# Cross-attention kernel: the low part of the context columns made by a negating copy on ScalarE and an accumulating DMA, in place of three VectorE subtractions

## Chip, cores and metric

One core of a Trainium2 chip runs the program. The metric is the device time of one execution in microseconds (us). The kernel before took 1278.85 us (median of three runs, 1278.84 to 1280.06).

## What is computed

The reference is one cross-attention layer over 64 batch elements, each with 256 text rows x (512 wide) and 256 context rows (384 wide):

```
text_p  = H_l @ W_text  + b_text          # [256, 512]
audio_p = H_a @ W_audio + b_audio         # [256, 512]
Q = layer_norm(text_p,  g1, beta1);  K = layer_norm(audio_p, g2, beta2);  V = audio_p
alpha   = softmax(Q @ K^T / sqrt(512))
H_hyper = (alpha @ V) @ W_out + b_out
return layer_norm(H_hyper + H_l, g_out, beta_out)
```

Inputs and output are float32.

## The kernel before

The 64 batch elements are taken in pairs: 32 steps, and in each step all matrix work is done on 512 tokens. Steps 0, 1, 30 and 31 are written out; steps 2 to 29 are a loop whose body holds two steps (`run_steps`). Every engine has its own program, and all order between engines is by semaphores written out by hand; there is no planner. The order of the calls inside each engine's `step` is the order of its queue.

TensorE multiplies in a rounded 32-bit format. To keep the precision of float32, each operand is split in a high part (a rounded copy) and a low part (the value less its high part), and each product is three matmuls: high by high, high by low, low by high. The context columns `cT_in` (128 partitions, 3 chunks of 512 tokens, 768 KB) are such an operand: `cT_hi` and `cT_lo` feed the K projection, `project_k`, with which each step of TensorE begins.

Step i on TensorE: `project_k` (4 banks), `project_q` (4 banks) with `mean_squares` of K in the middle of bank 1, `probs_context` of step i-1, `output_part` of step i-1 with `mean_squares` of Q in between, and `scores`. So at the end of a step TensorE goes straight from the scores of step i to `project_k` of step i+1, which needs `cT_hi` and `cT_lo` of step i+1. In the kernel before `product` waits for them chunk by chunk, on `cT_split` (one count for each VectorE subtraction).

How the parts of the context columns come about in step i, for step i+1:

- ScalarE makes `cT_hi` chunks 0 and 1 (`cT_high`) behind `move_half` of K, in front of `y_norm(i-2, odd, 0)` and of `rstd_of` for K; chunk 2 late in the step, behind `xT_minus`.
- VectorE makes `cT_lo` (`cT_low`): chunk 0 in front of the four `k_norm`, chunk 1 behind the last `q_low`, chunk 2 in front of `maxima(i, 0)`.
- SyncE then loads `cT_in` for step i+2 (`load_cT`), behind a wait on `cT_split`; `store_p`, `load_p` and the other transfers of the step are queued behind that wait.

For x the kernel already does otherwise: ScalarE makes all of `xT_hi` and then `xT_lo = -xT_hi` (`xT_minus`), and a GpSimd DMA adds `xT_in` to it (`add_xT`, accumulating, 1024 KB), after which `xT_split` counts 16. Only in step 0 does VectorE subtract (`x0_low`). GpSimd's queue in a step: `scales` and `finish_y(.., 0)` of step i-2, `pair_squares`, `bias_x` (an accumulating DMA of 1024 KB that adds the output bias to y rows), `finish_y(.., 1)`, `add_xT`, four `split_c`, `finish_y(.., 2)` and `(.., 3)`.

The stretch of ScalarE's step that the prediction follows is: `move_half` of Q, `k_high(i, 3)`, `pc_high(j, 1)`, `pc_high(j, 2)`, `rstd_of` for Q. `pc_high` rounds two of three banks of the probabilities-by-context product; VectorE's `pc_low(j, 1)`, `pc_low(j, 2)`, `k_low(i, 3)`, then `q_norm` and `q_low` follow it, and `scores` waits for the four `q_low`.

Of the kernel before, what the change touches and what calls it, by code (L numbers as in the profile page):

```python
# [18 lines left out]
def cross_attention_kernel(nc, x_rows, xT, c_rows, cT, w_text, b_text, w_audio, b_audio, w_out, b_out,  # L19
# [13 lines left out]
    with ExitStack() as stack:  # L33
# [92 lines left out]
        k_moved, q_moved = sem("k_moved"), sem("q_moved")  # L126
        k_log, q_log, k_rstd, q_rstd = sem("k_log"), sem("q_log"), sem("k_rstd"), sem("q_rstd")
        xT_negated, x0_split = sem("xT_negated"), sem("x0_split")
        k_centred, k_squared = sem("k_centred"), sem("k_squared")
        q_centred, q_squared, y_normed = sem("q_centred"), sem("q_squared"), sem("y_normed")  # L130
        kT_hi_made, qT_hi_made = sem("kT_hi_made"), sem("qT_hi_made")
# [53 lines left out]
        def _(sp):  # L185
# [46 lines left out]

            def step(i, odd, first=False, last=False):
                if first:
                    wait_apart(sp, cT_split, CT)
                    load_cT(1)
                    sp.wait_ge(x0_split, DT)
                elif not last:
                    wait_apart(sp, xT_split, 16 * i)
                if last:  # L240
                    sp.wait_ge(xT_split, 16 * (N - 1))
                    sp.dma_start(last_rows[:], x_rows[N - 1]).then_inc(x_last, 16)
                else:
                    load_xT(i + 1)
                if first:
                    sp.wait_ge(wao_done, CT)
                elif isinstance(i, int) and i == 1:
                    sp.wait_ge(bao_done, 1)
                if not isinstance(i, int) or i >= 2:
                    for t in (0, 1):  # L250
                        store_y(i - 2, odd, t)
                if not isinstance(i, int) or i < N - 2:
                    wait_apart(sp, cT_split, CT * (i + 2))
                    load_cT(i + 2)
                if not last:
                    store_p(i)
                if not isinstance(i, int) or i >= 2:
                    for t in (2, 3):
                        store_y(i - 2, odd, t)
                if not last:  # L260
                    load_p(i)
                for t in range(0 if last else T):
                    if not isinstance(i, int) or i >= 2:
                        wait_apart(sp, stored[t], 16 * (i - 1))
                    load_x(i, odd, t)
# [16 lines left out]
        def _(pe):  # L282
# [19 lines left out]
            def project_k(i, h):  # L302

                if isinstance(i, int) and i == 0:
                    pe.wait_ge(waT_copied, h + 1)
                wait(pe, y_summed, T * (i - 2) + h + 1)
                cols = slice(h * P, (h + 1) * P)
                terms = [(wa_hi[:, d, cols], wa_lo[:, d, cols], cT_hi[:, d, :], cT_lo[:, d, :]) for d in range(CT)]
                at_begin = isinstance(i, int) and i == 0 and h == 0
                product(wide[h][:], terms, cT_split if h == 0 else None, CT * i,  # L310
                        wa_split if at_begin else None).then_inc(k_done, 1)

            def project_q(i, h, part=None):
# [189 lines left out]
        def _(act):  # L503
# [6 lines left out]
            def xT_minus(i):  # L510

                act.wait_ge(xT_hi_made, DT * (i + 1))
                nc.scalar.mul(xT_lo[:], xT_hi[:].bitcast(F32), -1.0).then_inc(xT_negated, 1)  # L513

            def c_high(i):
                act.wait_ge(c_loaded, 16 * (i + 1))
                wait(act, pc_done, CT * i)
                nc.scalar.copy(c_hi[:], c_kept[:]).then_inc(c_hi_made, 1)  # L518
# [118 lines left out]
            def step(i, odd, first=False, last=False):  # L637
# [14 lines left out]
                if not last:  # L652
                    cT_high(i + 1, 0)
                    cT_high(i + 1, 1)
                if late:
                    y_norm(i - 2, odd, 0)
                rstd_of(i, turn[0], k_var, k_log, k_rstd)
# [10 lines left out]
                    pc_high(j, 0)  # L668
                move_half(i, turn[1], q_summed, q_moved)
                k_high(i, 3)  # L670
                if first:
                    wao_high(0)
                    wao_high(1)
# [18 lines left out]
                    wao_high(2)  # L692
                if not last:
                    xT_minus(i + 1)
                    cT_high(i + 1, 2)
                c_high(i)
                if late:
                    y_norm(i - 2, odd, 2)
# [48 lines left out]
        def _(dve):  # L747
# [6 lines left out]

            def cT_low(i, d):
                dve.wait_ge(cT_hi_made, CT * i + d + 1)
                low(cT_lo[:, d, :], cT_in[:, d, :], cT_hi[:, d, :]).then_inc(cT_split, 1)

            def turn_p(j):

# [194 lines left out]
            def step(i, odd, first=False, last=False):  # L955
# [13 lines left out]
                if late:  # L969
                    y_gain(i - 2, odd, 1)  # L970
                    y_gain(i - 2, odd, 2)
                if not last:
                    cT_low(i + 1, 0)
                k_norm(i, 0)
                k_norm(i, 1)
                k_norm(i, 2)
# [27 lines left out]
                if first:  # L1004
                    wao_low(2)
                    make_bao()
                if not last:
                    cT_low(i + 1, 1)
# [3 lines left out]
                if not last:  # L1012
                    cT_low(i + 1, 2)
                maxima(i, 0)
                if last:
                    wide_sum(y_rows[1 - odd], j, 2)
# [58 lines left out]
        def _(pool):  # L1075
# [21 lines left out]
            def add_xT(i):  # L1097

                wait_apart(pool, xT_negated, i)
                nc.gpsimd.dma_start(xT_lo[:], xT_in[:], accum_op=ALU.add).then_inc(xT_split, 16)  # L1100

            def split_c(i, t):

                if t == 0:
# [47 lines left out]
            def step(i, odd, first=False, last=False):  # L1152
# [12 lines left out]
                    bias_x(j, 1 - odd)  # L1165
                if last:
                    bias_last()
                if late:
                    finish_y(i - 2, odd, 1)
                if not last:  # L1170
# [60 lines left out]
```

## Time and profile before

| | |
|---|---|
| median of three runs | 1278.85 us |
| profiled execution, its own time | 1279.1 us |
| its span, first to last instruction | 1277.3 us |
| mean granted TensorE clock | 0.997 |
| TensorE matmul busy | 1257.2 us, 98% |
| VectorE busy | 1078.8 us, 84% |
| ScalarE busy | 1054.7 us, 83% |
| GpSimd busy | 547.5 us, 43% |
| DMA moved | 253.53 MB, mean 198 GB/s |

In the rows PE is TensorE's matmul, PEld its weight load (which runs beside the matmul before it), DVE VectorE, ACT ScalarE, POOL GpSimd, SPq the queue of SyncE, and L523 line 523 of the kernel. Helpers that write one kind of instruction for many tiles have one line (L749 is every subtraction), so go by the names of the tiles. Names in the trace are merged for likewise named tiles: "score<-kT_hi,qT_hi" is the matmul of `scores`. A matmul's end is modelled, so the starts of matmuls and weight loads are what tells TensorE's pace.

### The profile page before, as it was taken

To read this page: it belongs to the slowest core of one execution; us is meant where nothing else is said; L and a number is where in the kernel's file an instruction comes from. 1 tells how busy PE (TensorE), PEld (TensorE's weight loads), DVE (VectorE), ACT (ScalarE), POOL (GpSimd) and SP (SyncE) were. 2 spreads that over 40 slices of the span, in tenths; PEclk is the share of its full clock that TensorE was granted. 3 is DMA by queue.
4 is the path that set the end of the run, shared out by engine and by line. 5 is a ranking of instruction groups with operands and counts; after the bars stand their busy time and mean duration, and the time that the engine had idled before them with its cause. 6 is when DMAs were issued, how large, how long until landed. Compare 5 with 4: busy or idle time off the path is not lost.

```text
span 1277.3 us, 22559 instructions
## 1 busy us (share of the span) xinstructions
PE 1257.2 (98%) x6648; PEld 1066.4 (83%) x6648; DVE 1078.8 (84%) x1726; ACT 1054.7 (83%) x1789; POOL 547.5 (43%) x545
## 2 busy tenths in 40 slices
PE   6999999999999999999999999999999999999997
PEld 5688888888888888888888888888888888888886
DVE  6678888988888988888888888888889888889888
ACT  6777888888888888888888888888888888888874
POOL 0113554335544335544345544345544355543356
PEclk9999999999999999999999999999999999999999
DMA  7257766768766678766678667688666687667693
GB/s 255 60 162 224 225 191 182 186 202 238 227 169 198 184 216 238 212 178 194 182 227 238 204 170 194 192 234 231 185 187 184 202 243 222 179 189 188 209 233 105
DMA packets 99013, 253.53 MB, mean 198 GB/s; under 512 B 12336, under 2 KB 28208, under 8 KB 90800
## 3 DMA queue, kind: packets, MB, share of 16 engines
q1 hardware_dynamic: 77632, 187.22, 41.8%
q0 software_dynamic: 21360, 66.06, 28.7%
q8 instruction: 10, 0.16, 0.1%
q14 instruction: 11, 0.09, 0.0%
HBM read 137.38 MB, written 49.81 MB: 147 GB/s over the span
## 4 chain that ended last, share of the span: by engine, by line
PE 96%; DVE 2%; ACT 1%; DMA 1%; SPq 1%; issue 0%; ACTq 0%; DVEq 0%
PE wide L326 9%; PE wide L327 9%; PE wide L325 9%; PE score L293 7%; PE score L292 7%; PE score L294 7%; PE wide L294 7%; PE wide L292 7%; PE wide L293 7%; PE wide L382 7%; PE wide L381 7%; PE wide L380 7%; PE turn L334 2%; PE turn L293 1%; PE turn L294 1%; PE turn L292 1%
## 5 line engine op out<-in xcount | busy, mean ns | idle before, releaser
L1123 POOL TENSOR_TENSOR y_rows<-y_rows,betao_row 128x512 f32<-128x512 f32 x120 | 167.0, 1391 | 337.9 <-ACT y_rows L585 226.3
L325 PE MATMUL wide<-xT_hi,wt_hi 128*128 128x512 f32 x512 | 202.5, 395 | 3.4 <-ACT k_cols L545 3.4
L326 PE MATMUL wide<-xT_lo,wt_hi 128*128 128x512 f32 x512 | 202.5, 396 | 0.0
L327 PE MATMUL wide<-xT_hi,wt_lo 128*128 128x512 f32 x512 | 202.5, 396 | 0.0
L292 PE MATMUL wide<-cT_hi,wa_hi 128*128 128x512 f32 x384 | 151.7, 395 | 0.7 <-DVE wa_lo L924 0.7
L544 ACT ACTIVATE squares<-wide,bac_col 128x512 f32<-128x512 f32 x128 | 88.3, 690 | 77.2 <-PE wide L294 77.0
L294 PE MATMUL wide<-cT_hi,wa_lo 128*128 128x512 f32 x384 | 151.6, 395 | 0.0
L293 PE MATMUL wide<-cT_lo,wa_hi 128*128 128x512 f32 x384 | 151.3, 394 | 0.0
L382 PE MATMUL wide<-wao_hi,pcT_lo 128*128 128x512 f32 x372 | 146.7, 394 | 0.0
L380 PE MATMUL wide<-wao_hi,pcT_hi 128*128 128x512 f32 x372 | 146.6, 394 | 0.0
L381 PE MATMUL wide<-wao_lo,pcT_hi 128*128 128x512 f32 x372 | 146.5, 394 | 0.0
L292 PE MATMUL score<-kT_hi,qT_hi 128*128 128x256 f32 x512 | 145.3, 284 | 1.0 <-DVE qT_lo L825 1.0
L294 PE MATMUL score<-kT_hi,qT_lo 128*128 128x256 f32 x512 | 144.7, 283 | 0.0
L293 PE MATMUL score<-kT_lo,qT_hi 128*128 128x256 f32 x512 | 144.7, 283 | 0.0
L1106 POOL TENSOR_TENSOR c_lo<-c_kept,c_hi 128x384 fp32r<-128x384 f32 x128 | 126.1, 1011 | 19.5 <-ACT c_hi L518 19.5
L1100 POOL DMA_DIRECT2D xT_lo<-xT_in x31 | 27.8, 897 | 233.7 <-ACT xT_lo L513 233.7
L325 PEld LDWEIGHTS wide<-xT_hi,wt_hi 128*128 128x128 f32 x512 | 96.9, 189 | 25.6 <-ACT k_cols L545 4.3
L326 PEld LDWEIGHTS wide<-xT_lo,wt_hi 128*128 128x128 f32 x512 | 96.7, 189 | 22.8
L327 PEld LDWEIGHTS wide<-xT_hi,wt_lo 128*128 128x128 f32 x512 | 96.8, 189 | 22.4
L576 ACT ACTIVATE qT_hi<-q_cols,beta_col 128x512 fp32r<-128x512 f32 x128 | 90.7, 725 | 28.1 <-DVE q_cols L819 25.4
L825 DVE SCALAR_TENSOR_TENSOR qT_lo<-q_cols,beta_col,qT_hi 128x512 fp32r<-128x512 f32 x128 | 102.6, 801 | 8.5
L819 DVE SCALAR_TENSOR_TENSOR q_cols<-q_cols,g_col,turn 128x512 f32<-128x512 f32 x128 | 92.0, 740 | 12.4 <-ACT turn L567 12.4
(145 smaller groups left out, 3515.6 us busy)
## 6 DMA issues: line engine op xcount, KB each, us to landing
xT_in<-in_xT SPq DMA_DIRECT2D x32, 1024.0 KB, 9.0
xT_lo<-xT_in POOLq DMA_DIRECT2D x31, 1024.0 KB, 8.9
y_rows<-in_x_rows SPq DMA_DIRECT2D x124, 256.0 KB, 4.0
y_rows<-bao_row POOLq DMA_DIRECT2D x31, 1024.0 KB, 9.4
out<-y_rows SPq DMA_DIRECT2D x124, 256.0 KB, 3.3
cT_in<-in_cT SPq DMA_DIRECT2D x32, 768.0 KB, 8.7
c_kept<-in_c_rows SPq DMA_DIRECT2D x32, 768.0 KB, 7.5
p_out<-probs SPq DMA_DIRECT2D x31, 512.0 KB, 4.6
```

Of the source, the lines that this page charges most:

```text
L292: nc.tensor.matmul(to, a_hi, b_hi, start=(m == 0), stop=False)
L293: nc.tensor.matmul(to, a_hi, b_lo, start=False, stop=False)
L294: done = nc.tensor.matmul(to, a_lo, b_hi, start=False, stop=(m == n - 1))
L325: nc.tensor.matmul(wide[h][:], wt_hi[:, d, cols], xT_hi[:, d, :], start=(d == 0), stop=False)
L326: nc.tensor.matmul(wide[h][:], wt_hi[:, d, cols], xT_lo[:, d, :], start=False, stop=False)
L327: done = nc.tensor.matmul(wide[h][:], wt_lo[:, d, cols], xT_hi[:, d, :], start=False, stop=(d == DT - 1))
L380: nc.tensor.matmul(wide[t][:], hi, wao_hi[:, d, :], start=(d == 0), stop=False)
L381: nc.tensor.matmul(wide[t][:], hi, wao_lo[:, d, :], start=False, stop=False)
L382: done = nc.tensor.matmul(wide[t][:], lo, wao_hi[:, d, :], start=False, stop=(d == CT - 1))
L825: nc.vector.scalar_tensor_tensor(out=lo[:, h, :], in0=cols[:, h, :], scalar=shift[:, h:h + 1], in1=hi[:, h, :].bitcast(F32), op0=ALU.add, ...
L1106: nc.gpsimd.tensor_tensor(c_lo[:, t, :], c_kept[:, t, :], c_hi[:, t, :].bitcast(F32), ALU.subtract).then_inc(c_split, 1)
L1123: nc.gpsimd.tensor_tensor(rows, rows, betao_row[:], ALU.add).then_inc(y_ready, 1)
```

## The change

ScalarE makes the third chunk of `cT_hi` together with the other two, early in the step; `cT_minus`, one instruction over all three chunks (1536 elements in each partition), writes `-cT_hi` to `cT_lo` behind `k_high(i, 3)` and in front of `pc_high(j, 1)`; and a GpSimd DMA, `add_cT`, adds `cT_in` (768 KB) to it, queued between `bias_x` and `finish_y(i-2, odd, 1)`. The three VectorE subtractions of each step but the last are gone. Columns of step 0 are still split by VectorE, under a semaphore of their own, `c0_split`. `cT_split` now counts 16 for each DMA; TensorE waits for it once, ahead of `project_k(i, 0)`, and SyncE waits for it ahead of `load_cT`.

```
--- before.py
+++ after.py
@@ -126,6 +126,7 @@
         k_moved, q_moved = sem("k_moved"), sem("q_moved")
         k_log, q_log, k_rstd, q_rstd = sem("k_log"), sem("q_log"), sem("k_rstd"), sem("q_rstd")
         xT_negated, x0_split = sem("xT_negated"), sem("x0_split")
+        cT_negated, c0_split = sem("cT_negated"), sem("c0_split")
         k_centred, k_squared = sem("k_centred"), sem("k_squared")
         q_centred, q_squared, y_normed = sem("q_centred"), sem("q_squared"), sem("y_normed")
         kT_hi_made, qT_hi_made = sem("kT_hi_made"), sem("qT_hi_made")
@@ -232,7 +233,7 @@
 
             def step(i, odd, first=False, last=False):
                 if first:
-                    wait_apart(sp, cT_split, CT)
+                    sp.wait_ge(c0_split, CT)
                     load_cT(1)
                     sp.wait_ge(x0_split, DT)
                 elif not last:
@@ -250,7 +251,7 @@
                     for t in (0, 1):
                         store_y(i - 2, odd, t)
                 if not isinstance(i, int) or i < N - 2:
-                    wait_apart(sp, cT_split, CT * (i + 2))
+                    wait_apart(sp, cT_split, 16 * (i + 1))
                     load_cT(i + 2)
                 if not last:
                     store_p(i)
@@ -307,7 +308,9 @@
                 cols = slice(h * P, (h + 1) * P)
                 terms = [(wa_hi[:, d, cols], wa_lo[:, d, cols], cT_hi[:, d, :], cT_lo[:, d, :]) for d in range(CT)]
                 at_begin = isinstance(i, int) and i == 0 and h == 0
-                product(wide[h][:], terms, cT_split if h == 0 else None, CT * i,
+                if h == 0 and not at_begin:
+                    pe.wait_ge(cT_split, 16 * i)
+                product(wide[h][:], terms, c0_split if at_begin else None, 0,
                         wa_split if at_begin else None).then_inc(k_done, 1)
 
             def project_q(i, h, part=None):
@@ -512,6 +515,11 @@
                 act.wait_ge(xT_hi_made, DT * (i + 1))
                 nc.scalar.mul(xT_lo[:], xT_hi[:].bitcast(F32), -1.0).then_inc(xT_negated, 1)
 
+            def cT_minus(i):
+
+                act.wait_ge(cT_hi_made, CT * (i + 1))
+                nc.scalar.mul(cT_lo[:], cT_hi[:].bitcast(F32), -1.0).then_inc(cT_negated, 1)
+
             def c_high(i):
                 act.wait_ge(c_loaded, 16 * (i + 1))
                 wait(act, pc_done, CT * i)
@@ -652,6 +660,7 @@
                 if not last:
                     cT_high(i + 1, 0)
                     cT_high(i + 1, 1)
+                    cT_high(i + 1, 2)
                 if late:
                     y_norm(i - 2, odd, 0)
                 rstd_of(i, turn[0], k_var, k_log, k_rstd)
@@ -668,6 +677,8 @@
                     pc_high(j, 0)
                 move_half(i, turn[1], q_summed, q_moved)
                 k_high(i, 3)
+                if not last:
+                    cT_minus(i + 1)
                 if first:
                     wao_high(0)
                     wao_high(1)
@@ -692,7 +703,6 @@
                     wao_high(2)
                 if not last:
                     xT_minus(i + 1)
-                    cT_high(i + 1, 2)
                 c_high(i)
                 if late:
                     y_norm(i - 2, odd, 2)
@@ -754,7 +764,7 @@
 
             def cT_low(i, d):
                 dve.wait_ge(cT_hi_made, CT * i + d + 1)
-                low(cT_lo[:, d, :], cT_in[:, d, :], cT_hi[:, d, :]).then_inc(cT_split, 1)
+                low(cT_lo[:, d, :], cT_in[:, d, :], cT_hi[:, d, :]).then_inc(c0_split, 1)
 
             def turn_p(j):
 
@@ -969,8 +979,6 @@
                 if late:
                     y_gain(i - 2, odd, 1)
                     y_gain(i - 2, odd, 2)
-                if not last:
-                    cT_low(i + 1, 0)
                 k_norm(i, 0)
                 k_norm(i, 1)
                 k_norm(i, 2)
@@ -1004,13 +1012,9 @@
                 if first:
                     wao_low(2)
                     make_bao()
-                if not last:
-                    cT_low(i + 1, 1)
                 if not first:
                     y_sum(j, 1 - odd, 0)
                     y_sum(j, 1 - odd, 1)
-                if not last:
-                    cT_low(i + 1, 2)
                 maxima(i, 0)
                 if last:
                     wide_sum(y_rows[1 - odd], j, 2)
@@ -1099,6 +1103,11 @@
                 wait_apart(pool, xT_negated, i)
                 nc.gpsimd.dma_start(xT_lo[:], xT_in[:], accum_op=ALU.add).then_inc(xT_split, 16)
 
+            def add_cT(i):
+
+                wait_apart(pool, cT_negated, i)
+                nc.gpsimd.dma_start(cT_lo[:], cT_in[:], accum_op=ALU.add).then_inc(cT_split, 16)
+
             def split_c(i, t):
 
                 if t == 0:
@@ -1165,6 +1174,8 @@
                     bias_x(j, 1 - odd)
                 if last:
                     bias_last()
+                if not last:
+                    add_cT(i + 1)
                 if late:
                     finish_y(i - 2, odd, 1)
                 if not last:
```

## Rows read from the trace of the kernel before

**Rows 1.** The page: engines (busy us, share, instructions); chain that ended last.

```profile
PE 1257.2 (98%) x6648; PEld 1066.4 (83%) x6648; DVE 1078.8 (84%) x1726; ACT 1054.7 (83%) x1789; POOL 547.5 (43%) x545
PE 96%; DVE 2%; ACT 1%; DMA 1%; SPq 1%; issue 0%; ACTq 0%; DVEq 0%
```

**Rows 2.** Waits of TensorE: us in total, times, longest us.

```profile
PE wide L325 <- ACT k_cols L545: 3.4, 2, 2.0
...
PE score L292 <- DVE qT_lo L825: 1.0, 2, 0.7
```

**Rows 3.** Groups by line, whole trace: busy us, mean ns, idle before.

```profile
L749 DVE TENSOR_TENSOR cT_lo<-cT_in,cT_hi 128x512 fp32r<-128x512 f32 x96 | 66.0, 687 | 25.6 <-ACT cT_hi L523 25.6
...
L513 ACT ACTIVATE xT_lo<-xT_hi 128x2048 fp32r<-128x2048 f32 x31 | 59.4, 1916 | 1.0
...
L518 ACT CAST c_hi<-c_kept 128x1536 fp32r<-128x1536 f32 x32 | 47.2, 1475 | 0.0
```

**Rows 4.** Timeline of ScalarE in a loop step: start us, duration us, [idle before].

```profile
608.46 1.14 ACT L523 CAST cT_hi<-cT_in 128x512 fp32r<-128x512 f32 x2
...
611.00 0.66 ACT L565 ACTIVATE turn<-turn,eps 128x512 f32<-128x512 f32 x1 [0.77 <-PE turn L334]
...
621.44 0.57 ACT L539 CAST pcT_hi<-score 128x512 fp32r<-128x512 f32 x1
622.32 0.59 ACT L539 CAST pcT_hi<-turn 128x512 fp32r<-128x512 f32 x1 [0.32 <-PE turn L294]
623.94 0.66 ACT L565 ACTIVATE turn<-turn,eps 128x512 f32<-128x512 f32 x1 [1.03 <-PE turn L334]
```

**Rows 5.** Timeline of VectorE in the same step.

```profile
622.89 0.69 DVE L749 TENSOR_TENSOR pcT_lo<-score,pcT_hi 128x512 fp32r<-128x512 f32 x1
...
624.10 0.74 DVE L825 SCALAR_TENSOR_TENSOR kT_lo<-k_cols,beta_col,kT_hi 128x512 fp32r<-128x512 f32 x1
625.25 1.41 DVE L819 SCALAR_TENSOR_TENSOR q_cols<-q_cols,g_col,turn 128x512 f32<-128x512 f32 x2 [0.40 <-ACT turn L567]
...
630.55 0.75 DVE L825 SCALAR_TENSOR_TENSOR qT_lo<-q_cols,beta_col,qT_hi 128x512 fp32r<-128x512 f32 x1
```

**Rows 6.** Timeline of TensorE's weight loads in the same step.

```profile
610.46 0.19 PEld L334 LDWEIGHTS turn<-sq_parts,mean_of 128*128 128x128 f32 x1 [0.36 <-DVE sq_parts L749]
...
624.89 0.19 PEld L380 LDWEIGHTS wide<-wao_hi,pcT_hi 128*128 128x128 f32 x1
...
631.65 0.19 PEld L292 LDWEIGHTS score<-kT_hi,qT_hi 128*128 128x128 f32 x1
...
636.33 0.19 PEld L292 LDWEIGHTS wide<-cT_hi,wa_hi 128*128 128x128 f32 x1
```

**Rows 7.** Timeline of GpSimd in the same step.

```profile
616.53 1.35 POOL L1113 DMA_DIRECT2D y_rows<-bao_row  x1 [1.13 <-DMA y_rows<-in_x_rows]
625.93 1.30 POOL L1123 TENSOR_TENSOR y_rows<-y_rows,betao_row 128x512 f32<-128x512 f32 x1 [8.04 <-ACT y_rows L585]
```

**Rows 8.** DMA: landing of all 31 of line L1100 (xT_lo); the page's line of y_rows (KB each, us).

```profile
DMA to landing us min/median/max: 7.0/8.9/11.6
y_rows<-bao_row POOLq DMA_DIRECT2D x31, 1024.0 KB, 9.4
```

**Rows 9.** Window: busy of PE, PEld, DVE, ACT, POOL, clock, DMA share, GB/s.

```profile
630.00:632.00 2.00, 2.00 (x15) 1.85 (x14) 1.87 (x4) 1.97 (x4) 0.00 (x0) 1.00 0.00 0
```

**Rows 10.** Steps 0 and 1: timelines of ScalarE, GpSimd, SyncE, TensorE, VectorE; landing of the one at 54.06.

```profile
38.46 0.72 ACT L571 ACTIVATE kT_hi<-k_cols,beta_col 128x512 fp32r<-128x512 f32 x1
...
54.06 1.07 POOL L1100 DMA_DIRECT2D xT_lo<-xT_in  x1 [20.28 <-ACT xT_lo L513]
...
54.73 0.33 SPq L187 DMA_DIRECT2D cT_in<-in_cT  x1
...
65.74 0.47 PE L325 MATMUL wide<-xT_hi,wt_hi 128*128 128x512 f32 x1 [1.42 <-ACT k_cols L545]
...
67.82 0.69 DVE L749 TENSOR_TENSOR sq_parts<-sq_half,sq_parts 64x512 fp32r<-64x512 f32 x1
...
DMA to landing us min/median/max: 11.6/11.6/11.6
```

More of the change, by code:

```diff
@@ L128, in cross_attention_kernel @@
         xT_negated, x0_split = sem("xT_negated"), sem("x0_split")
+        cT_negated, c0_split = sem("cT_negated"), sem("c0_split")
         k_centred, k_squared = sem("k_centred"), sem("k_squared")
@@ L234, in step @@
                 if first:
-                    wait_apart(sp, cT_split, CT)
+                    sp.wait_ge(c0_split, CT)
                     load_cT(1)
@@ L252, in step @@
                 if not isinstance(i, int) or i < N - 2:
-                    wait_apart(sp, cT_split, CT * (i + 2))
+                    wait_apart(sp, cT_split, 16 * (i + 1))
                     load_cT(i + 2)
@@ L309, in project_k @@
                 at_begin = isinstance(i, int) and i == 0 and h == 0
-                product(wide[h][:], terms, cT_split if h == 0 else None, CT * i,
+                if h == 0 and not at_begin:
+                    pe.wait_ge(cT_split, 16 * i)
+                product(wide[h][:], terms, c0_split if at_begin else None, 0,
                         wa_split if at_begin else None).then_inc(k_done, 1)
@@ L513, in xT_minus, with cT_minus @@
                 nc.scalar.mul(xT_lo[:], xT_hi[:].bitcast(F32), -1.0).then_inc(xT_negated, 1)
+            def cT_minus(i):
+                act.wait_ge(cT_hi_made, CT * (i + 1))
+                nc.scalar.mul(cT_lo[:], cT_hi[:].bitcast(F32), -1.0).then_inc(cT_negated, 1)
             def c_high(i):
@@ L654, in step @@
                     cT_high(i + 1, 1)
+                    cT_high(i + 1, 2)
                 if late:
@@ L670, in step @@
                 k_high(i, 3)
+                if not last:
+                    cT_minus(i + 1)
                 if first:
@@ L694, in step @@
                     xT_minus(i + 1)
-                    cT_high(i + 1, 2)
                 c_high(i)
@@ L756, in cT_low @@
                 dve.wait_ge(cT_hi_made, CT * i + d + 1)
-                low(cT_lo[:, d, :], cT_in[:, d, :], cT_hi[:, d, :]).then_inc(cT_split, 1)
+                low(cT_lo[:, d, :], cT_in[:, d, :], cT_hi[:, d, :]).then_inc(c0_split, 1)
             def turn_p(j):
@@ L971, in step @@
                     y_gain(i - 2, odd, 2)
-                if not last:
-                    cT_low(i + 1, 0)
                 k_norm(i, 0)
@@ L1006, in step @@
                     make_bao()
-                if not last:
-                    cT_low(i + 1, 1)
                 if not first:
@@ L1011, in step @@
                     y_sum(j, 1 - odd, 1)
-                if not last:
-                    cT_low(i + 1, 2)
                 maxima(i, 0)
@@ L1100, in add_xT, with add_cT @@
                 nc.gpsimd.dma_start(xT_lo[:], xT_in[:], accum_op=ALU.add).then_inc(xT_split, 16)
+            def add_cT(i):
+                wait_apart(pool, cT_negated, i)
+                nc.gpsimd.dma_start(cT_lo[:], cT_in[:], accum_op=ALU.add).then_inc(cT_split, 16)
             def split_c(i, t):
@@ L1167, in step @@
                     bias_last()
+                if not last:
+                    add_cT(i + 1)
                 if late:
```

## The prediction

> **What bounds the kernel now.** I read the page's engine shares and its chain first. TensorE is busy for 98% of the span and holds 96% of the chain that ended last; VectorE, from which the change takes work, holds 2% of it [rows 1]. Then the waits, TensorE's alone: in 1277.3 us it stood idle for 3.4 us ahead of the Q projection (two times) and 1.0 us ahead of the scores (two times, both in the last step), and in no loop step at all [rows 2]. So VectorE time is not worth anything by itself. The change can only cost time, by making something that TensorE needs late in a loop step, or save it at one of the few places where TensorE does wait. Third I read the timelines of one loop step, to see how early each thing arrives that the change touches. Every loop step that I looked at shows the same idle times to 0.01 us ahead of ScalarE's two `rstd_of`, so one step stands for the 28 of the loop and nearly for steps 1 and 30.
>
> **What is removed.** Three subtractions in 31 of 32 steps; the group of 96 (three of them step 0's own, which stay) took 687 ns each, with 25.6 us of waiting for `cT_hi` beside them [rows 3]. That is 93 x 0.687 = 64 us of VectorE, 2.1 us in each step, all of it beside a busy TensorE: 0 us off the time. At the end of a step it lets `maxima` and the exponentials run some 0.4 us earlier, but those of the next K bank wait for TensorE anyway: also 0.
>
> **The third `cT_hi` chunk, moved up.** Two chunks take 1.14 us, so the third adds 0.57 us ahead of K's `rstd_of`. There ScalarE idles 0.77 us for TensorE's mean matmul [rows 4]. It fits with 0.20 us to spare: 0. Without that cover each 0.1 us would come off the K chain, which is itself tight at one point only (the mean matmul's load at 610.46 waits 0.36 us for VectorE's parts [rows 6]), and that point lies before the moved chunk. `cT_in` has long landed: it was loaded in the step before.
>
> **The negation.** 1536 elements on ScalarE. A rounding copy of that size takes 1475 ns; the same operation as mine with a third more elements takes 1916 ns, three quarters of which is 1437 ns [rows 3]. I take 1.48 us; overlapped with its neighbour it delays the next instruction by about 1.4 us. It stands where `pc_high(j, 1)` starts at 621.44. Behind it ScalarE has idle times of 0.32 and 1.03 us before Q's `rstd_of` at 623.94 [rows 4], 1.35 us together. So `rstd_of` starts at most 0.05 us late.
>
> What is queued behind it: `pc_high(j, 1)` now starts near 622.83 and ends near 623.4, so VectorE's `pc_low(j, 1)` starts at about 623.45 and not at 622.89, 0.55 us late. VectorE has 0.40 us idle ahead of `q_norm` [rows 5]: it starts Q's normalization 0.05 to 0.15 us late. Two users of this work on TensorE: `output_part` for chunk 1 has its weights loaded at 624.89 [rows 6], and needs `pc_low(j, 1)`, now done near 624.15, 0.7 us ahead; chunk 2 is 0.7 us later on both sides. And the last `q_low`: it starts at 630.55 and ends at 631.30, and the weight load that needs it is at 631.65 [rows 5, 6]. That is the narrowest place: 0.35 us of room, of which the change eats 0.05 to 0.15. Cost 0, with 0.2 us left. Beyond the room each 0.1 us would cost 0.1 x 30 steps = 3 us. Ends of the unknown: -0 (nothing on this path waits less), and, if the negation took the full 1916 ns of the longer row, 0.45 us more delay, 0.2 over the room, 30 x 0.2 = 6 us.
>
> **The accumulating DMA.** Issued by GpSimd at about 622.95, when the negation is done. GpSimd has nothing to do there: it waited 8.04 us ahead of `finish_y(.., 1)` at 625.93 [rows 7], and an issue of this kind takes about 0.9 to 1.4 us, so it is through at 624.3 and `finish_y` starts as before. `bias_x`, issued at 616.53 and landing 9.4 us later, at 625.9, is ahead of it in the same queue [rows 7, 8]. The nearest rows are 1024 KB accumulations, at 7.0, 8.9 and 11.6 us [rows 8]. Lower bound: three quarters of the least, 5.3 us, landing at 628.2. Upper bound: the longest in full, counted from the issue, 634.6; or the median in full counted from the landing of `bias_x`, 634.8. I take 631: the DMA engines move nothing in 630 to 632 today [rows 9], so it has them to itself once the bias is through. TensorE needs the result for the weight load at 636.33 [rows 6]: 5 us of room, 1.5 us at the upper bound. Cost 0 at both ends. The Trainium skill (DMA: Bandwidth & Descriptors, Anatomy of one DMA) gives a DMA about 2.0 us fixed plus bytes over 436 GB/s, which for 768 KB would be an estimate of 3.8 us. The trace does not agree: its accumulations of 1024 KB, 4.4 us by that rule, took 7.0 us at the least; but by the rule as by the rows the sum is the same, 0.
>
> SyncE's `load_cT` was released by the last subtraction, near 634.7; now by the landing near 631. Its load then runs in the gap of [rows 9] and is partly out of the way when `add_xT` is issued at 634.1; nothing on SyncE's queue becomes later. The single wait that TensorE now makes replaces three, in a queue that runs ahead: 0.
>
> **Where something is gained: step 1.** TensorE waited 1.42 us ahead of the first Q matmul at 65.74. The view names ScalarE, but that work ended long before; what ended there was `add_xT`, issued at 54.06 and landing 11.6 us later, at 65.7 [rows 10]. It is the slowest of the 31 (median 8.9 [rows 8]), because `load_cT(2)`, issued at 54.73 [rows 10], and the probability store came in with it on idle DMA engines. After the change, in step 0 the negation runs behind `k_high(0, 3)` (38.46 + 0.63 = 39.1 to 40.6), the accumulation lands at about 46 to 50, and `load_cT(2)` starts then, and is done by 54 to 58. `add_xT` at 54.06 should then take 7.0 to 9.3 us and land at 61.1 to 63.4; TensorE comes for it at 65.74 - 1.42 - some 0.1 = 64.2. So the wait goes whole, 1.4 us. What is late next is the K mean matmul: its parts are done at 67.82 + 0.69 = 68.5 [rows 10], and TensorE, 1.4 us earlier, asks at 68.4: it loses 0.1 of the gain at most. I take -1.4 us.
>
> **Sum.** 0 for 28 loop steps and for steps 30 and 31, -1.4 us in step 1: the profiled execution 1279.1 us would be 1277.7; the median 1278.85 lies 0.25 lower, so 1277.4 us.
>
> **Rivals.**
> (a) The last `q_low` becomes the bound of each step. The Q chain is moved by more than the 0.35 us of room; the point from which it decides is a delay of Q's `rstd_of` or of `pc_low(j, 1)` 0.2 us longer than I worked out. For it: the room of ScalarE, 1.35 us, and the negation are equal to 0.05 us. Against: even 0.1 us of error leaves room. At 0.15 us over the room, 30 x 0.15 = 4.5 us, less 1.4: 1282.0 us; slower. Chance 9%.
> (b) `cT_lo` lands too late. GpSimd's queue holds it behind `bias_x`, and in some steps the landing passes 636.33. Against: the upper bound is 1.5 us earlier. 1 us late in each of 30 steps is +30 us, 1307 us. Chance 2%.
> (c) The step 1 wait stays, since something other than the collision (the first use of the queue, say) made that DMA slow. For it: it is also the first accumulating DMA of all. In the changed kernel `add_cT(1)` is the first. Time as before, 1278.9 us. Chance 17%.
> (d) The relief of VectorE and ScalarE also takes away what TensorE loses at the K mean load in each step, where the load waits 0.36 us [rows 6]; half of that, taken as lost to the matmuls, is 31 x 0.18 = 5.6 us, 1271.8 us with step 1. Against: its chain starts from TensorE's own last K bank, and ScalarE and VectorE wait at each of its links. Chance 3%.
> My forecast: 69%.
>
> **How the numbers follow.** A measurement of this kernel can tell about 0.2%, 2.6 us, from no change. Forecast and (c) lie within it: 86%. Slower is (a) and (b), less the small overruns of (a) that stay within 0.2%: 9%. Faster is (d) and what I have not seen: 5%. The range runs from a little below the forecast, 1276.2 (a step 1 gain twice as large), to 1282.0, rival (a) with its price; it leaves out the 6 us end of the negation, (b) and (d).
>
> **What would show it.** The first Q matmul of step 1 near 64.3 without an idle time, and the landing of the first xT accumulation under 9.5 us. In a loop step: ScalarE idle about 0.2 us ahead of K's `rstd_of` and under 0.1 us ahead of Q's; the negation at 1.48 us; a landing of `cT_lo` 6 to 9 us after its issue; no TensorE wait on `cT_split`, on `pcT_lo` or on `qT_lo`. Wrong it would be if the weight load of the fourth score product showed a wait in every step (rival a), the first K load one (rival b), or if the period of a loop step changed at all.

## The result, and the profile after

The changed kernel took 1277.66 us (median of 20 runs), the kernel before 1279.28 us (median of 20 beside them); ratio 0.9987, 95% interval 0.9981 to 0.9993, that is 0.9 to 2.4 us less. Forecast were 1277.4 us and a gain of 1.4 us. It lies within the 0.2% that was called no change. The runs of either kernel fall in two groups 1.5 us apart (told below), some 10 of 20 in the upper one before and 5 of 20 after; group by group the gain is 1.2 us, and the rest of the 1.6 between the medians is that share.

The page, engines and chain, against [rows 1]:

```profile
PE 1258.7 (99%) x6648; PEld 1067.2 (84%) x6648; DVE 1048.7 (82%) x1633; ACT 1096.4 (86%) x1820; POOL 563.4 (44%) x576
PE 95%; DVE 3%; ACT 1%; DMA 1%; SPq 1%; issue 0%; DVEq 0%; ACTq 0%
```

ScalarE gained 42 us (31 negations). TensorE's busy time rose by 1.5 us in a span that is the same to 0.1, which comes from stretches at its lower clock in step 0, told below. VectorE lost only 30 us of busy time, though the 93 subtractions that went were 64 as the prediction counts them. Each overlaps the next record by some 0.08 us, so 56 us of the engine's time went; and 26 us came back at one other instruction, told at the end. The waits of TensorE, against [rows 2]:

```profile
PE turn L337 <- DVE sq_parts L759: 2.1, 1, 2.1
...
PE score L293 <- DVE qT_lo L835: 1.0, 2, 0.7
PE wide L328 <- ACT k_cols L553: 0.6, 1, 0.6
```

The wait ahead of the Q projection, 3.4 us in two places before, is 0.6 us in one: that of step 1 is gone. All of these lie in steps 0 and 31. The groups of the moved work, against [rows 3]:

```profile
L521 ACT ACTIVATE cT_lo<-cT_hi 128x1536 fp32r<-128x1536 f32 x31 | 45.6, 1471 | 0.0
...
L759 DVE TENSOR_TENSOR cT_lo<-cT_in,cT_hi 128x512 fp32r<-128x512 f32 x3 | 2.1, 687 | 0.9 <-ACT cT_hi L531 0.9
```

One loop step on ScalarE, against [rows 4]. Times in it are 0.18 us later than those of before (the K mean's weight load stands at 610.64 and not at 610.46):

```profile
608.64 1.66 ACT L531 CAST cT_hi<-cT_in 128x512 fp32r<-128x512 f32 x3
...
611.18 0.66 ACT L573 ACTIVATE turn<-turn,eps 128x512 f32<-128x512 f32 x1 [0.25 <-PE turn L337]
...
621.62 1.47 ACT L521 ACTIVATE cT_lo<-cT_hi 128x1536 fp32r<-128x1536 f32 x1
623.00 0.56 ACT L547 CAST pcT_hi<-score 128x512 fp32r<-128x512 f32 x1
623.47 0.58 ACT L547 CAST pcT_hi<-turn 128x512 fp32r<-128x512 f32 x1
624.12 0.66 ACT L573 ACTIVATE turn<-turn,eps 128x512 f32<-128x512 f32 x1
```

Each `rstd_of` begins with a logarithm (the rows at 611.18 and 624.12). The idle times ahead of the two have shrunk, 0.77 to 0.25 us and 1.03 to under 0.1, and neither logarithm is later: 624.12 less 0.18 is 623.94, as before. VectorE and the weight loads of the same step, against [rows 5, 6]:

```profile
623.60 0.69 DVE L759 TENSOR_TENSOR pcT_lo<-score,pcT_hi 128x512 fp32r<-128x512 f32 x1 [0.55 <-ACT pcT_hi L547]
...
625.46 1.40 DVE L829 SCALAR_TENSOR_TENSOR q_cols<-q_cols,g_col,turn 128x512 f32<-128x512 f32 x2
...
630.73 0.75 DVE L835 SCALAR_TENSOR_TENSOR qT_lo<-q_cols,beta_col,qT_hi 128x512 fp32r<-128x512 f32 x1
```

```profile
610.64 0.19 PEld L337 LDWEIGHTS turn<-sq_parts,mean_of 128*128 128x128 f32 x1 [0.35 <-DVE sq_parts L759]
...
631.84 0.19 PEld L293 LDWEIGHTS score<-kT_hi,qT_hi 128*128 128x128 f32 x1
...
636.51 0.19 PEld L293 LDWEIGHTS wide<-cT_hi,wa_hi 128*128 128x128 f32 x1
```

The idle 0.40 us in front of Q's normalization has moved ahead of `pc_low(j, 1)`; the normalization is 0.03 us later. The last `q_low` ends at 631.48, 0.36 us ahead of its weight load (0.35 before). The accumulating DMA on GpSimd, its landing, and SyncE's load behind it, against [rows 7, 8]:

```profile
623.69 0.88 POOL L1109 DMA_DIRECT2D cT_lo<-cT_in  x1 [6.82 <-ACT cT_lo L521]
626.11 1.30 POOL L1132 TENSOR_TENSOR y_rows<-y_rows,betao_row 128x512 f32<-128x512 f32 x1 [1.54 <-ACT y_rows L593]
```

```profile
DMA to landing us min/median/max: 5.7/5.8/6.5
```

```profile
629.78 0.35 SPq L188 DMA_DIRECT2D cT_in<-in_cT  x1
```

The accumulation of the context columns lands at 629.5, 7 us ahead of TensorE's need at 636.51, and releases the load about 5 us earlier than before. The load then has the DMA engines nearly to itself, and so has the x accumulation after it. The page's DMA lines (x accumulation 8.9 before, `cT_in` 8.7):

```profile
xT_lo<-xT_in POOLq DMA_DIRECT2D x31, 1024.0 KB, 6.9
...
cT_in<-in_cT SPq DMA_DIRECT2D x32, 768.0 KB, 4.3
```

Steps 0 and 1, against [rows 10]: SyncE, GpSimd, the landing of that DMA, and TensorE's first Q matmul of step 1, without an idle time:

```profile
49.26 0.33 SPq L188 DMA_DIRECT2D cT_in<-in_cT  x1
```

```profile
55.59 0.87 POOL L1104 DMA_DIRECT2D xT_lo<-xT_in  x1 [11.75 <-ACT xT_lo L516]
```

```profile
DMA to landing us min/median/max: 7.0/7.0/7.0
```

```profile
65.72 0.39 PE L328 MATMUL wide<-xT_hi,wt_hi 128*128 128x512 f32 x1
```

**Why the two profiled executions have the same span.** 1277.3 us before and 1277.4 us after, though the medians differ by 1.6 us. In both kernels the runs fall in two groups about 1.5 us apart (before near 1278.85 and 1280.4, after near 1277.6 and 1279.2), and the profiled execution of before was of the lower group, that of after (1279.22 us) of the upper. The windows show what separates them. Columns: PE, PEld, DVE, ACT, POOL, granted clock, DMA share, GB/s. Before:

```profile
24.00:26.00 2.00, 2.00 (x6) 1.52 (x6) 1.93 (x4) 1.39 (x3) 0.00 (x0) 0.50 0.45 126
30.00:32.00 2.00, 2.00 (x10) 1.62 (x9) 1.41 (x3) 2.00 (x4) 0.00 (x0) 1.00 0.00 0
```

After:

```profile
24.00:26.00 2.00, 2.00 (x9) 1.43 (x8) 1.93 (x4) 1.42 (x3) 0.00 (x0) 1.00 0.50 113
30.00:32.00 2.00, 2.00 (x6) 1.61 (x5) 1.33 (x3) 1.80 (x5) 0.00 (x0) 0.50 0.00 0
```

At the start TensorE waits for weights and data, and has a stretch at the lower of its two clocks (1.2 GHz). Before, the stretch covered 24 to 26 us, where the K mean at 28.7 hid it. After, it covered 30 to 32 us, where nothing hides it: step 0's Q mean started at 44.11 instead of 42.54, 1.57 us later. From there to the K mean of step 1 it took 27.47 us before and 26.01 after, 1.46 less. So the gain of step 1 is in this trace in full, next to a start that had nothing to do with it.

The other traces bear this out. Of the 13 kernels timed here, seven have a stretch at the lower clock between 28 and 34 us (the changed one, e1, e2, e4, e6, e8, e9), and in these step 0's Q mean starts at 43.6 to 44.1 us. In the other six it lies at 22 to 27 us (before, e5, e7) or there is none in step 0 (e3, e10, e11), and the Q mean starts at 42.1 to 42.6. Step 0's K mean starts at 28.5 to 28.8 in all of them. e1 and e9 hold nothing of the change, so the change does not make the late stretch.

### The profile page after: what moved, and what is told of

It is laid out like the page before. It is cut to its first block, busy times and chain, and to the rows that moved or that the text cites. A ratio compares the mean times of both kernels' runs of the same rounds, so it can differ in the third digit from the quotient of the medians.

```text
span 1277.4 us, 22446 instructions
## 1 busy us (share of the span) xinstructions
PE 1258.7 (99%) x6648; PEld 1067.2 (84%) x6648; DVE 1048.7 (82%) x1633; ACT 1096.4 (86%) x1820; POOL 563.4 (44%) x576
## 3 DMA queue, kind: packets, MB, share of 16 engines
q1 hardware_dynamic: 77632, 187.22, 42.6%
## 4 chain that ended last, share of the span: by engine, by line
PE 95%; DVE 3%; ACT 1%; DMA 1%; SPq 1%; issue 0%; DVEq 0%; ACTq 0%
PE wide L329 9%; PE wide L330 9%; PE wide L328 9%; PE score L294 7%; PE score L293 7%; PE score L295 7%; PE wide L295 7%; PE wide L293 7%; PE wide L294 7%; PE wide L385 7%; PE wide L384 7%; PE wide L383 7%; PE turn L337 2%; PE turn L294 1%; PE turn L295 1%; PE turn L293 1%
## 5 line engine op out<-in xcount | busy, mean ns | idle before, releaser
L1132 POOL TENSOR_TENSOR y_rows<-y_rows,betao_row 128x512 f32<-128x512 f32 x120 | 156.8, 1306 | 184.3 <-ACT turn L575 133.5
L1109 POOL DMA_DIRECT2D cT_lo<-cT_in x31 | 27.4, 884 | 205.9 <-ACT cT_lo L521 198.4
```

The source lines that it names most:

```text
L1132: nc.gpsimd.tensor_tensor(rows, rows, betao_row[:], ALU.add).then_inc(y_ready, 1)
```

## Experiments

Each was timed beside the kernel before on the same chip; the ratio is to that. The kernel before took 1279.71 us beside e1 to e4, 1280.12 beside e5 to e8 and 1279.02 beside e9 to e11, so compare the ratios and not the medians. "Loop step" is the mean distance of the K mean matmul from step to step, steps 1 to 30 of the profiled execution. "Into step 1" is the time from the Q mean matmul of step 0 to the K mean matmul of step 1: it holds the wait that the prediction is about, and not the stretch of step 0 that makes the two groups. In e4 and e9 this K mean stands one matmul later by the edit, and in e10 two.

| kernel | runs | median us | ratio to before (95%) | loop step us | into step 1 us |
|---|---|---|---|---|---|
| before | 20 | 1279.28 | 1 | 38.61 | 27.47 |
| changed | 20 | 1277.66 | 0.9987 (0.9981 to 0.9993) | 38.61 | 26.01 |
| e1 before, cT load late | 11 | 1277.58 | 0.9986 (0.9977 to 0.9995) | 38.60 | 26.02 |
| e2 changed, load with x | 11 | 1278.13 | 0.9987 (0.9978 to 0.9996) | 38.60 | 26.03 |
| e3 changed, VectorE work back | 11 | 1278.28 | 0.9987 (0.9978 to 0.9996) | 38.60 | 26.02 |
| e4 changed, K mean 1 later | 5 | 1271.27 | 0.9935 (0.9921 to 0.9949) | 38.42 | 26.04 |
| e5 changed, load at x | 11 | 1280.07 | 0.9998 (0.9989 to 1.0007) | 38.60 | 27.02 |
| e6 changed, small op | 10 | 1279.13 | 0.9991 (0.9981 to 1.0) | 38.62 | 26.01 |
| e7 changed, one copy moved | 10 | 1282.14 | 1.0024 (1.0014 to 1.0033) | 38.76 | 26.01 |
| e8 changed, two copies moved | 4 | 1297.36 | 1.0136 (1.0121 to 1.0152) | 39.28 | 26.03 |
| e9 before, K mean 1 later | 5 | 1274.52 | 0.9960 (0.9946 to 0.9973) | 38.41 | 27.44 |
| e10 changed, K mean 2 later | 5 | 1273.84 | 0.9957 (0.9944 to 0.9971) | 38.51 | 26.26 |
| e11 changed, late negation | 2 | 1413.69 and 1436.33 | | 43.02 (41.6 to 44.8) | 31.33 |

**Where the gain came from: e1, e2, e5.**

e1 leaves the kernel before as it is but for one wait of SyncE:

```
                     wait_apart(sp, cT_split, CT * (i + 2))
+                    if first:
+                        sp.wait_ge(xT_split, 16)
                     load_cT(i + 2)
```

> The kernel before, with one wait added: in step 0 SyncE loads the context columns of step 2 only when the first x accumulation has landed. Nothing of the change is in it. Theory (collision of that load with the first x accumulation cost TensorE 1.42 us in step 1): the accumulation, 11.6 us before, lands in 7 to 8 us, the first Q matmul of step 1 starts without an idle time, and the time is 1.2 to 1.6 us below the kernel before. Rival (c) (the first accumulating DMA of a run is slow by itself): it lands in about 11 us again and the time is that of the kernel before. The loop steps stay at 38.61 us by both.

The load went out at 63.28. The accumulation, still the first of the run, landed in 7.8 us, and TensorE did not wait:

```profile
DMA to landing us min/median/max: 7.8/7.8/7.8
```

```profile
65.58 0.39 PE L327 MATMUL wide<-xT_hi,wt_hi 128*128 128x512 f32 x1
```

The ratio is that of the whole change. So its gain can be had by one wait in step 0, with no VectorE or ScalarE work moved. Rival (c) is out: the first use of the queue costs at most the 0.8 us between 7.8 and the 7.0 of the changed kernel, and TensorE had room for that. The changed kernel says the same: there the first accumulation of the run is that of the context columns, and it took 6.4 us where the median of its 31 is 5.8.

The wait of e1 also holds back the probability store, which is behind the load in SyncE's queue (issued at 63.72; at 59.10 in the kernel before). So e1 by itself doesn't tell the load from the store. The changed kernel does: its store goes out 5.1 us behind the x accumulation, in the kernel before 5.0 behind, and the accumulation takes 7.0 us all the same.

e2 and e5 put the load back beside that accumulation in the changed kernel:

```
                     wait_apart(sp, cT_split, 16 * (i + 1))
+                    if first:
+                        sp.wait_ge(xT_negated, 1)      # e2;  e5: sp.wait_ge(neg_max_made, 1)
                     load_cT(i + 2)
```

> The changed kernel, with one wait added: in step 0 SyncE loads the context columns of step 2 only when the x columns of step 1 are negated, so that the load again meets the first x accumulation. All else of the change stays. Theory: that accumulation takes 10 to 12 us instead of 7.0, TensorE waits 1 to 2 us ahead of the first Q matmul of step 1, and the whole gain of the change is gone (within 0.3 us of the kernel before). Rival (the gain comes from relieved VectorE or ScalarE): the time stays 1.2 to 1.6 us below the kernel before.

e2 failed as a test of the time: the collision came back, but only in part. The load was issued at 54.94, 0.59 us ahead of the accumulation (55.53), which landed in 10.0 us, at 65.5; TensorE came at 65.67 and did not wait. The gain stayed, as the rival had it. e2 alone therefore doesn't part the two; but its accumulation shows why nothing was lost: the price of the meeting, 3.0 us, had fitted in TensorE's room.

```profile
DMA to landing us min/median/max: 10.0/10.0/10.0
```

> The changed kernel, with step 0's load of the context columns of step 2 held back until the first score maximum of step 0 is made. That puts its issue about 0.4 us behind the first x accumulation's, as in the kernel before (0.67 us behind); in e2_after_collision_back it was 0.59 us ahead, the accumulation took 10.0 us and TensorE did not wait. Theory: which of the two comes first decides what the meeting costs: the accumulation lands in 10.5 to 11.5 us, TensorE waits 0.3 to 1.3 us in step 1, and that much of the gain goes. Rival: the first use of the queue made the rest of the 11.6 us (it was the first accumulating DMA before and is the second here): 10.0 us again, no wait, time of the changed kernel.

The load came at 53.75, 0.19 us ahead of the accumulation at 53.94, and not 0.4 us behind as I had worked out; it landed in 11.1 us, and TensorE waited:

```profile
DMA to landing us min/median/max: 11.1/11.1/11.1
```

```profile
65.19 0.47 PE L330 MATMUL wide<-xT_hi,wt_hi 128*128 128x512 f32 x1 [0.96 <-DMA xT_lo<-xT_in]
```

With all of the moved work still moved, the way into step 1 is 27.02 us, so 1.0 of the 1.46 us is lost again; the ratio, 0.9998, says the same but can't tell 1.0 from 1.46. Here the view names the DMA itself, which in [rows 10] it put down to ScalarE. By the order of issue the accumulation took 7.0 us (load 6.3 us ahead), 10.0 (0.59 ahead), 11.1 (0.19 ahead), and in the kernel before 11.6 (0.67 behind, and the first of its run; e9 repeats it, 11.3 at 0.67 behind). In all of them the store follows the accumulation by 5.0 to 5.1 us. Why so little in the order counts for so much was not tried.

**VectorE's time: e3.**

```
+            def busy(n):
+                nc.vector.reduce_max(spare[:, n:n + 1], wt_hi[:, 0, :].bitcast(F32), AX_X)
...
+                    busy(0)      # ahead of k_norm(i, 0)
...
+                    busy(1)      # ahead of y_sum(j, 1 - odd, 0)
...
+                    busy(2)      # ahead of maxima(i, 0)
```

> The changed kernel, with three VectorE instructions of about 0.68 us put back where the three subtractions stood in each step (each reduces 512 elements of the weights to one maximum that nothing uses; only the time of the three subtractions is given back, not their waits for ScalarE). Theory (VectorE time is worth nothing under TensorE): same time as the changed kernel to 0.3 us, loop step 38.61 us. Rival (the relief of VectorE brought the gain): 1.2 us or more above the changed kernel.

Same ratio as the changed kernel, same loop step: three instructions of 0.68 us in each step, 63 us of VectorE, cost nothing that can be measured. What the change took off VectorE was worth 0. (The waits of the three subtractions for ScalarE are not given back in e3.)

**The room of the Q chain: e6, e7, e8.** In e6 a copy of 16 elements stands behind the negation; in e7 and e8 rounding copies of x go there from between the `q_high`:

```
                 if not last:
                     cT_minus(i + 1)
+                    xT_high(i + 1, 0)      # e7 and e8
+                    xT_high(i + 1, 1)      # e8
```

> The changed kernel, with one more ScalarE instruction behind the negation in every step but the last (16 elements, copied to a scratch tile that nothing uses, about 0.2 us). First point of three that measure the room of the Q chain: the last low part of Q is done 0.36 us ahead of the weight load that needs it. Theory: 0.2 us fits, loop step 38.61 us, time unchanged to 0.5 us. Rival (a) (the chain was already at its end): +0.2 us in each of 30 steps, 6 us.

> The changed kernel, with one 512-element rounding copy of the x columns moved from between the Q copies to right behind the negation: 0.57 us more ahead of Q's logarithm, no work added. Theory (room 0.36 us, VectorE has no idle time left in front of Q's normalization): 0.57 - 0.36 = 0.21 us in each of 30 steps, loop step 38.8 us, +6 us over the changed kernel. Rival (the room is larger than the weight load shows, or the order of the copies makes it good again): under 1 us.

> The changed kernel, with two of these copies moved: 1.14 us more ahead of Q's logarithm. Theory: 1.14 - 0.36 = 0.78 us in each of 30 steps, loop step 39.4 us, +23 us over the changed kernel. Rival (TensorE's wait is taken at the output matmuls, whose low parts come late too, and not twice): same total, but the wait stands ahead of the output matmul of chunk 1. Without any bound by this chain: no change.

e6 changed nothing, but it is a weak point: the copy took 0.19 us and moved the next instruction by 0.09 only. In e7 the logarithm of Q came at 624.93, no idle time ahead of it, and Q's normalization 0.51 us later against the K mean than in the changed kernel. The loop step grew by 0.145 us, 0.06 us less than expected, so the room is 0.51 - 0.145 = 0.365 us, about the 0.36 us that the weight load shows. Taken at the end of the last `q_low`, 0.47 us later, it is 0.33. The step grew by less than expected because the moved copy of 0.57 us delayed the normalization by 0.51 only. It came out at the one place named in the prediction, the weight load of the fourth score product:

```profile
632.35 0.39 PE L293 MATMUL score<-kT_hi,qT_hi 128*128 128x256 f32 x1
```

That matmul started 0.17 us behind its neighbour and the next 0.22 us behind it, where 0.12 is the pace. This is rival (a), built: 30 x 0.145 = 4.4 us. In e8 the loop step grew by 0.67 us (0.78 expected; the normalization is 1.04 us later and not 1.14, and 1.04 - 0.67 = 0.37). The wait stands at both users of the stretch, so neither reading had it whole. By the starts of the matmuls some 0.2 us of it are lost at the output matmul of chunk 1 and 0.5 at the fourth score product:

```profile
PE score L293 <- DVE qT_lo L833: 7.5, 31, 0.7
...
PEld score L293 <- DVE qT_lo L833: 14.4, 33, 0.9
...
PEld wide L383 <- DVE pcT_lo L757: 10.5, 30, 0.4
```

**Too late a low part: e11.**

```
                 if not last:
+                    cT_minus(i + 1)
                     xT_minus(i + 1)
...
                 if late:
                     finish_y(i - 2, odd, 1)
                 if not last:
+                    add_cT(i + 1)
                     add_xT(i + 1)
```

> The changed kernel, with the negation of the context columns put off to the end of the step, right ahead of the negation of the x columns, and their accumulating DMA right ahead of that of x. It prices rival (b), a low part that lands too late. Working: negation done 633.2 us on the scale of the loop step shown, issue 633.8, landing 5.8 us later at 639.6, needed at 636.5: TensorE waits 3.1 us ahead of the K projection in each step, loop step 41.7 us, time about 1277.5 + 31 x 3.1 = 1374 us. If a low part that lands late were hidden by anything, it would be less.

It took 1413.69 and 1436.33 us, with a mean granted clock of 0.963 and 0.944. The wait is 2.8 us (3.1 worked out) in each of 31 steps of the profiled execution, that of 1413.69 us:

```profile
PE wide L293 <- DMA cT_lo<-cT_in: 87.7, 31, 3.8
```

but the time rose by 136 us and not by 96. The rest is in TensorE's busy time, 1306.0 us instead of 1258.7. After the wait (TensorE busy 1.24 of 4 us) the granted clock fell:

```profile
648.00:652.00 4.00, 1.24 (x9) 1.00 (x8) 2.39 (x4) 3.39 (x11) 3.98 (x5) 1.00 1.08 213
652.00:656.00 4.00, 4.00 (x13) 3.14 (x12) 2.23 (x8) 1.27 (x2) 3.92 (x4) 0.61 1.18 197
```

Some of the steps took 41.6 us, near the 41.7 worked out; others 43.2 or 44.4, with stretches at the lower clock. So rival (b) would have been dearer than the 30 us that I gave it for 1 us a step, if its waits were as long as these.

**A faster kernel: e4, e9, e10.** The one wait for another engine that the view of the loop steps shows is that of the K mean's weight load, 0.36 us [rows 6].

```
                     nc.tensor.matmul(wide[h][:], wt_hi[:, d, cols], xT_hi[:, d, :], start=(d == 0), stop=False)
+                    if mean is not None and d == 2:
+                        mean()
...
-                mean_squares(i, turn[0][:], k_sq_parts, k_var)
-                project_q(i, 1, 2)
+                project_q(i, 1, 2, lambda: mean_squares(i, turn[0][:], k_sq_parts, k_var))
```

> The changed kernel, with TensorE's mean matmul of K put one matmul (0.23 us) later, behind the first matmul of the third chunk of Q bank 1. Now its weight load waits 0.35 us for VectorE in each step. Theory (that wait costs TensorE about 0.2 us in each of 31 steps and nothing else is bound): loop step 38.61 becomes 38.40 to 38.50 us, the load waits 0.1 us or so, and the time falls by 3.5 to 6 us below the changed kernel. Rival (the wait is hidden by the matmuls in flight, or the later mean makes ScalarE late by more than its 0.25 us of room): loop step 38.6 us or more, time the same or higher.

```profile
607.28 0.40 PE L328 MATMUL wide<-xT_hi,wt_hi 128*128 128x512 f32 x1
607.52 0.40 PE L339 MATMUL turn<-sq_parts,mean_of 128*128 128x512 f32 x1
607.75 0.40 PE L331 MATMUL wide<-xT_lo,wt_hi 128*128 128x512 f32 x1
```

The mean now stands in TensorE's even pace of 0.23 us, in the changed kernel the matmul starts around it are 0.31 and 0.34 us apart. 38.61 - 38.42 = 0.19 us, 31 times: 5.9 us. Ratio 0.9935, the fastest of all that were run: 6.6 us less than the changed kernel by the ratios, 5.7 less where the lower group of e4 is set beside those of e2 and e3.

> The kernel before, with TensorE's mean matmul of K one matmul later (as in e4, where the loop step fell from 38.61 to 38.41 us), and nothing of the change. Theory (the wait of that weight load has nothing to do with the work that the change moved): loop step 38.41 us here too, 6.2 us below the kernel before, and still the wait of 1.4 us in step 1, so 1.2 to 1.4 us above e4. Rival (d) (part of that gain needs the relieved VectorE or ScalarE): less than 5 us.

The loop step falls by the same 0.2 us in the kernel before, so rival (d) is out: that loss has nothing to do with VectorE's load. The wait of step 1 is still there (1.17 us). The ratio 0.9960 is 5.1 us (3.5 to 6.9 by its interval), which by itself can't tell the 6.2 expected from the rival's less than 5; with five runs the two groups of the start weigh in. The loop step decides.

> The changed kernel, with the mean matmul of K two matmuls later instead of one. Theory (one matmul later already hides all of that weight load's wait; the pace of 38.41 us is that of TensorE alone): loop step 38.41 us again, time within 0.5 us of e4; ScalarE's room of 0.3 us ahead of K's logarithm is used up, which the Q chain takes within its own room. Rival: K's logarithm later by 0.2 us comes out at the scores, loop step 38.5 us or more, 3 us above e4.

Two matmuls later is 0.09 us a step worse than one, 2.8 us by the ratios: the rival was right, and the theory missed. The mean itself costs nothing more, but a score matmul of each step starts 0.19 us behind its neighbour instead of 0.12. Against the scores K's logarithm is 0.2 us later, and so is all that ScalarE does behind it, because nothing idles ahead of Q's logarithm any more (0.03 us). The last `q_low` now ends 0.05 us ahead of the weight load of the fourth score product, against 0.17 in e4 and 0.35 in the changed kernel. In e9, where ScalarE still idles 1.03 us ahead of Q's logarithm, it is 0.36. So the change and the moved mean draw on the same room.

## Why the prediction was right

- The bound. TensorE alone sets the loop step: shown by 38.61 us in both kernels, and by e3. But "in no loop step at all" was read too strictly from the waits: e4 shows that TensorE lost 0.19 us at each K mean, in two gaps too short for that view. Rival (d) had the size (0.18 us); the change gives none of it back, and the load still waits 0.35 us. So the sum was not touched by it.
- The third chunk moved up. Forecast: 0.20 us of idle time left ahead of K's logarithm; measured 0.25.
- The negation. Forecast 1.48 us and a logarithm of Q at most 0.05 us late; measured 1.471 us and 0.00. Q's normalization: forecast 0.05 to 0.15 us late, measured 0.03. The room at the last weight load was read as 0.35 us before the change; e7 measured 0.33 to 0.365.
- The DMA. Landing forecast at 631, bounds 628.2 and 634.8; measured 629.5, which is 629.3 on the scale of before. Two errors cancelled in part: GpSimd's issue starts 0.6 us behind the end of the negation (623.09 to 623.69), not at once, and the transfer took 5.8 us and not 8, also less than the 6 to 9 named as a sign. The lower bound from the rows, 5.3 us, came close. The estimate of 3.8 us by the Trainium skill (DMA: Bandwidth & Descriptors, Anatomy of one DMA) was further off.
- Step 1. Forecast: the wait of 1.42 us goes whole because `load_cT(2)` no longer meets the first x accumulation; measured 1.46 us between the two means. The first Q matmul starts at 65.72, in an execution of the upper group; less the 1.57 us of its start that is 64.15, where 64.3 was forecast. Up to there 1.59 us are gained and 0.13 are lost again ahead of the K mean, as the prediction had it (0.1). e1 shows the cause with nothing else changed, e5 takes it away with all else changed. The landing of 7.0 us was the lower end of the 7.0 to 9.3 that I gave. The load went out at 49.26, inside 46 to 50.
- Not foreseen: that step 0 has two lengths 1.5 us apart, as large as the gain itself. The median of before shown ahead of the prediction, 1278.85 of three runs, was of the lower group; over 20 runs it was 1279.28. So the step from 1277.4 to the measured 1277.66 holds no test of the sum to better than some 0.5 us, and that the two agree to 0.3 is in part luck. The test is the 1.46 us in the traces.

## What to carry to other kernels

On a kernel that one engine bounds in every step, as here, work taken off another engine is worth nothing by itself; ask instead what the move triggers earlier or later, and look at the few places where the bound engine waits. There the releaser that the view names may have ended long before; look for the DMA that landed at that moment, and test it with one added wait. The room of a chain can be read off as the distance from its last result to the weight load that needs it, and filled to that; the cheapest gain here was not in the change at all, but in moving one small matmul behind a matmul that was ready. Work that fits is still not free: the change took ScalarE's idle time, and the room that is left for a second change is smaller for it (0.17 us in e4).

## What was not expected of the hardware

- One VectorE instruction became twice as long. `pair_squares` of K (L783 before, L793 after) went from 788 to 1598 ns, 26 us in all:

```profile
L793 DVE TENSOR_TENSOR squares<-squares 128x512 f32<-128x512 f32 x32 | 51.1, 1598 | 11.4 <-ACT squares L552 11.4
```

It starts at 603.11, just behind a GpSimd addition of 603.03 to 604.32, and ends 0.54 us behind that one. Timelines of VectorE and of GpSimd:

```profile
603.11 1.75 DVE L793 TENSOR_TENSOR squares<-squares 128x512 f32<-128x512 f32 x1 [0.31 <-ACT squares L552]
```

```profile
603.03 1.29 POOL L1132 TENSOR_TENSOR y_rows<-y_rows,betao_row 128x512 f32<-128x512 f32 x1
```

In the kernel before, VectorE came first and GpSimd's addition was the longer one:

```profile
602.97 0.89 DVE L783 TENSOR_TENSOR squares<-squares 128x512 f32<-128x512 f32 x1
```

```profile
603.38 1.62 POOL L1123 TENSOR_TENSOR y_rows<-y_rows,betao_row 128x512 f32<-128x512 f32 x1
```

The Trainium skill (SBUF — State Buffer, SBUF: two separate sides) says that a VectorE operation with two SBUF inputs and a GpSimd operation that reads SBUF exclude each other for a whole instruction, by who starts first; the trace agrees: 0.69 us of work took the rest of the GpSimd instruction, 1.21 us, and 0.54 more. It cost no time here, since the next `add_square` waits for ScalarE still.

VectorE's lighter load is not the cause. In e3 VectorE has its time back and the instruction is as long:

```profile
L797 DVE TENSOR_TENSOR squares<-squares 128x512 f32<-128x512 f32 x32 | 50.8, 1588 | 11.4 <-ACT squares L553 11.4
```

What decides is who starts first. On the scale of before, GpSimd's addition starts at 602.85 and not at 603.38, 0.53 us earlier in this and every loop step looked at, while VectorE's instruction starts earlier by 0.04 us (by 0.4 in every other step). By the timelines it comes from ScalarE, whose rounding copy `c_high` starts 0.5 us earlier since the third `cT_hi` chunk no longer stands in front of it, and GpSimd's `split_c` and additions follow that copy; this was not tried by itself.

- Two DMAs of 1024 and 768 KB that were issued within a microsecond of each other took longer by their order: the accumulation 10.0, 11.1 or 11.6 us with the load 0.59 us ahead, 0.19 ahead or 0.67 behind, and 7.0 where the load had landed before.
- After waits of some 2.8 us in each step the granted clock fell in the stretch behind them (0.61 in one window of 4 us), and cost 47 us over the run of e11, half of what the waits themselves cost (88 us).
- The length of step 0 changes by 1.5 us from run to run with the place of one stretch at the lower clock (the 13 traces above).
